# Delta-rule attention with a mixture-of-experts layer: VectorE's side work placed between filter taps, and a merge level of the block inverse in factored form

## The reference, cut to what matters

```python
# x: (8, 1024, 128); q: 8 heads; k, v: 8 heads x 3 householder steps per token; head size 128
q = _short_conv(x @ Wq, conv_q); k = _short_conv(x @ Wk, conv_k); v = _short_conv(x @ Wv, conv_v)
# _short_conv: y[t] = silu(sum of 4 taps w[i] * x[t - 3 + i])
q = _l2norm(q) * d ** (-0.5); k = _l2norm(k)
def step(S, inp):                       # scan over the 1024 tokens
    S = S * jnp.exp(gt)[..., None, None]
    for i in range(nh):                 # 3 rank-1 updates per token
        kS = jnp.einsum('bhd,bhde->bhe', ki, S)
        S = S + bi[..., None, None] * (ki[..., None] * (vi - kS)[:, :, None, :])
    return S, jnp.einsum('bhd,bhde->bhe', qt, S)
o = o * jax.lax.rsqrt(jnp.mean(o * o, -1, keepdims=True) + 1e-05) * rms_weight
x = _layernorm(x + (o * jax.nn.silu(gate)).reshape(b, t, h * dv) @ Wo)
# then a layer of 8 experts with top-2 weights, and a second _layernorm
```

## Time and profile before

| | |
|---|---|
| time, median of 3 runs | 8508.51 us (8502.43 to 8517.87) |
| the profiled execution: own time, span | 8499.04 us, 8497.0 us |
| busy in the span: PE, DVE, ACT, POOL | 7561.9, 6595.7, 5290.1, 4106.0 us |
| mean granted clock of TensorE | 0.956 of full speed |

### The profile page before, as it was taken

One profiled execution on the slowest core, in us unless ns is written; L12 is line 12 of the kernel. 1 busy time (PEld: TensorE's weight loads), 2 busy tenths in 40 slices (PEclk: granted clock), 3 DMA queues, 4 the chain that ended last, 5 costly groups with the idle time before them and its releaser, 6 DMA issues. The chain is left out here.

```text
span 8497.0 us, 425999 instructions
## 1 busy us (share of the span) xinstructions
PE 7561.9 (89%) x155940; PEld 6383.7 (75%) x155940; DVE 6595.7 (78%) x22297; ACT 5290.1 (62%) x19575; POOL 4106.0 (48%) x6333
## 2 busy tenths in 40 slices
PE   5788988888889888888888889889898889979999
PEld 1677777777777777777777777777777777857777
DVE  3888888888888888888888888888888888733333
ACT  2566666666666666666666666666666666623333
POOL 0355555555555555555555555555555555511111
PEclk6799999999999999999999999999999999989999
DMA  2000000000000000000000000000000000010000
GB/s 86 5 9 9 9 10 9 9 9 9 10 9 10 9 9 9 9 10 9 10 10 9 10 9 9 10 8 10 9 9 9 10 9 10 8 29 10 7 10 8
DMA packets 283622, 97.66 MB, mean 11 GB/s; under 512 B 226096, under 2 KB 276544, under 8 KB 281152
## 3 DMA queue, kind: packets, MB, share of 16 engines
q1 hardware_dynamic: 281408, 68.93, 3.7%
HBM read 52.08 MB, written 16.78 MB: 8 GB/s over the span
## 5 line engine op out<-in xcount | busy, mean ns | idle before, releaser
L802 DVE SCALAR_TENSOR_TENSOR CY<-PP,CWV,CY 128x128 f32<-128x128 f32 x4608 | 1590.3, 345 | 102.2 <-ACT CY L721 1.4
L802 DVE SCALAR_TENSOR_TENSOR CY<-PP,CWK,CY 128x128 f32<-128x128 f32 x4608 | 1587.4, 344 | 83.9
L1004 POOL TENSOR_TENSOR UM<-U,C 32x256 f32<-32x256 f32 x1536 | 1104.8, 719 | 120.2 <-POOL UM L1004 20.8
L997 POOL TENSOR_TENSOR Y<-U,C 32x256 f32<-32x256 f32 x768 | 553.9, 721 | 1201.0 <-DVE UQ L880 1160.9
L516 PE MATMUL PP<-XT,WK 128*128 128x131 f32 x3072 | 741.5, 327 | 262.0 <-DVE CY L802 251.5
L516 PE MATMUL PP<-XT,WV 128*128 128x131 f32 x3072 | 756.6, 333 | 239.8 <-DVE CY L802 212.3
L977 POOL TENSOR_TENSOR S<-R,BETA 96x4 f32<-96x4 f32 x512 | 101.4, 198 | 1606.6 <-DVE R L840 1606.6
L536 PE MATMUL PI<-T,WB 32*32 32x32 f32 x49152 | 732.6, 194 | 138.7 <-DVE T L811 133.7
L536 PEld LDWEIGHTS PI<-T,WB 32*32 32x32 f32 x49152 | 623.2, 109 | 298.6 <-issue 230.2
L721 ACT ACTIVATE CY<-PP,CWK 128x128 f32<-128x128 f32 x1536 | 560.7, 365 | 453.8 <-PE PP L516 447.4
L820 DVE SCALAR_TENSOR_TENSOR S<-S,WHOLE,PK 128x128 f32<-128x128 f32 x2048 | 612.6, 341 | 253.1 <-PE PK L591 252.9
(11 more groups left out here) (228 smaller groups left out, 19080.8 us busy)
## 6 DMA issues: line engine op xcount, KB each, us to landing
EX<-exd SPq DMA_DIRECT2D x768, 32.0 KB, 2.2
exd<-EXS SPq DMA_DIRECT2D x16, 512.0 KB, 2.6
XR<-in_L_attn_x SPq DMA_DIRECT2D x65, 64.0 KB, 2.7
XL<-in_L_attn_x SPq DMA_DIRECT2D x16, 256.0 KB, 2.8
XRES<-in_L_attn_x SPq DMA_DIRECT2D x64, 64.0 KB, 3.0
x<-X SPq DMA_DIRECT2D x64, 64.0 KB, 1.6
XI<-x SPq DMA_DIRECT2D x16, 256.0 KB, 2.8
out<-OUT SPq DMA_DIRECT2D x16, 256.0 KB, 2.3
```

The source lines that it names most:

```text
L802: dve.scalar_tensor_tensor(CY[:, m % RING], ptile(m)[:, s:s + P], taps_of(m)[:, s:s + 1], CY[:, m % RING], ALU.mult, ALU.add).then_inc(tap ...
L997: pool.tensor_tensor(Y1[r, :, :], U[r, par, :, r], over(first[r, :], [BK, NHEAD, BK], 1), ALU.mult).then_inc(seed_sb, 1)
L1004: pool.tensor_tensor(UM[r, lv], U[r, par, :, r], over(merge[lv][r, :], [BK, NHEAD, BK], 1), ALU.mult).then_inc(made, 1)
```

## The change

Four things, all in the attention stage.

1. A merge level of the inverse is computed as P = X - N X, Q = N P, result = P + N Q, in place of T0 = X - N X, T1 = X - N T0, result = X - N T1. The matmul blocks are the same in number and size. Q is a plain copy out of PSUM, and ScalarE makes it (steps 2 and 6, ahead of its slot's other work); VectorE keeps steps 1, 3, 5 and 7.
2. VectorE's passes of the inverse move from ahead of tap 1 to between taps 1 and 2, the transposes behind them to between taps 2 and 3. The reciprocal of the row norms moves from behind their sum to between taps 2 and 3. The second half of the state's addition is spread over slots 0 and 1, one head in each gap. QSE moves one gap later.
3. TensorE issues `new_state` in slots 10 and 11 in place of 11 and 12.
4. The norm's work of slot 12 in c = 2 is spread: YL in slot 13, statistics in slots 0 and 1 of c = 3, X1 in slot 4 in place of slot 1. GpSimd's root for it moves from the end of c = 2 to behind the first block of c = 3.

```diff
@@ stage_bufs
-                    "H1": (base, T0, T1),
-                    "H2": (base, T1, (Y2, Y3)[k // 4])}[STAGES[k]]
+                    "H1": (None, T0, T1),
+                    "H2": (T0, T1, (Y2, Y3)[k // 4])}[STAGES[k]]
@@ TensorE's program
-                        if k in (11, 12) and do_run:
-                            new_state(k - 11, run, rc, prep, do_prep)
+                        if k in (10, 11) and do_run:
+                            new_state(k - 10, run, rc, prep, do_prep)
@@ ScalarE's program
-                        if do_inv and k in INV_AT and INV_AT[k] in (0, 4):
+                        if do_inv and k in INV_AT and INV_AT[k] in (0, 2, 4, 6):
                             act.wait_ge(inv_ps, STEPS * invn + INV_AT[k] + 1)
-                            act.activation(WB[:, :, :], inv, ACT.Copy).then_inc(inv_sb, 1)
+                            to = WB if INV_AT[k] in (0, 4) else T1
+                            act.activation(to[:, :, :], inv, ACT.Copy).then_inc(inv_sb, 1)
@@ inv_out
-                    dve.tensor_tensor(to[:, :, :], base[:, :, :], inv, ALU.subtract).then_inc(inv_sb, 1)
+                    dve.tensor_tensor(to[:, :, :], base[:, :, :], inv, ALU.subtract if STAGES[k] == "H" else ALU.add).then_inc(inv_sb, 1)
@@ VectorE's group(i, half, c, k, part)
-                    if k == 0 and known(run - 1, 0, NCH):
-                        add_state(1, run - 1, part)
+                    if do_inv and k in INV_AT and INV_AT[k] not in (0, 2, 4, 6) and part == 0:
+                        inv_out(invn, INV_AT[k])
+                    if do_inv and INV_AT.get(k) == 3 and part == 1:
+                        dve.wait_ge(inv_sb, STEPS * invn + 4)
+                        flip(XB, Y2).then_inc(x2t_sb, 1)
...
+                    if k in (0, 1) and known(run - 1, 0, NCH):
+                        add_state(1, run - 1, 2 * k + part, 4)
                     if k in (3, 5) and do_prep and part == 0:
...
+                    if k in (3, 5) and do_prep and part == 1:
+                        l = k // 5
                         dve.wait_ge(sse_sb, 2 * prep + l + 1)
                         need(dve, kds_sb, 2 * prep - 1 + l)
                         dve.reciprocal(R2[0:R, lanes[l]], SSE[0:R, lanes[l]]).then_inc(r2_sb, 1)
-                    if k == 10 and c == 3 and do_prep and part == 0:
+                    if k == 10 and c == 3 and do_prep and part == 1:
...
-                    if k == 12 and out_now and part == 0:
+                    if k == 13 and out_now and part == 1:
...
-                        dve.wait_ge(y_sb, q + 1)
+                    if k == 0 and norm_now and part == 0:
+                        dve.wait_ge(y_sb, i - 1)
                         dve.bn_stats(ST[:, :], YL[:, :]).then_inc(st_sb, 1)
...
-                    if k == 1 and c == 3 and known(i - 2, 0, NSC) and part == 0:
+                    if k == 4 and norm_now and part == 1:
```

More of the change, by code:

```diff
@@ L459, in stage_bufs @@
             base = (Y1, Y2)[k // 4]
[L460 to L461 removed]
+            return {"W0": (base, None, None), "W1": (base, None, None), "H": (base, base, T0), "H1": (None, T0, T1),
+                    "H2": (T0, T1, (Y2, Y3)[k // 4])}[STAGES[k]]
         def when(i, c):
@@ L826, in group @@
                     ahead, prep, invn, run, do_ahead, do_prep, do_inv, do_run = when(i, c)
+                    norm_now = c == 3 and known(i - 2, 0, NSC)
                     rc, par = (c - 2) % 4, c % 2
@@ L830, in group @@
                     next_x = c == 3 and known(i + 1, 1, NSC)
-                    if k == 0 and known(run - 1, 0, NCH):
-                        add_state(1, run - 1, part)
+                    if do_inv and k in INV_AT and INV_AT[k] not in (0, 2, 4, 6) and part == 0:
[3 more added lines that the diff above has]
+                        flip(XB, Y2).then_inc(x2t_sb, 1)
+                    if do_inv and INV_AT.get(k) == 7 and part == 1:
+                        dve.wait_ge(inv_sb, STEPS * invn + 8)
+                        need(dve, join_ps, 3 * (invn - 1) + 1)
+                        for b in range(2):
+                            r = slice(BK * b, BK * b + BK)
+                            op = dve.transpose(X3[r, :, r], Y3[r, :, :])
+                        op.then_inc(x3t_sb, 1)
+                    if k in (0, 1) and known(run - 1, 0, NCH):
+                        add_state(1, run - 1, 2 * k + part, 4)
                     if k in (3, 5) and do_prep and part == 0:
@@ L881, in group @@
                     if k == 11 and do_run:
-                        add_state(0, run, part)
-                    if k == 12 and out_now and part == 0:
+                        add_state(0, run, part, 2)
+                    if k == 13 and out_now and part == 1:
                         q = i - 2
@@ L911, in program @@
                     for k in range(SLOTS):
-                        if do_inv and k in INV_AT and INV_AT[k] not in (0, 4):
-                            inv_out(invn, INV_AT[k])
-                            if INV_AT[k] == 3:
-                                dve.wait_ge(inv_sb, STEPS * invn + 4)
-                                flip(XB, Y2).then_inc(x2t_sb, 1)
-                            if INV_AT[k] == 7:
-                                dve.wait_ge(inv_sb, STEPS * invn + 8)
-                                need(dve, join_ps, 3 * (invn - 1) + 1)
-                                for b in range(2):
-                                    r = slice(BK * b, BK * b + BK)
-                                    op = dve.transpose(X3[r, :, r], Y3[r, :, :])
-                                op.then_inc(x3t_sb, 1)
                         j, jh, m = lagged(i, half, SLOTS * c + k - 1)
@@ L968, in program @@
                             pool.wait_ge(diag_sb, NBK * run + b + 1)
+                    if c == 3 and known(i - 2, 0, NSC):
+                        pool.wait_ge(mv_sb, 2 * (i - 1))
+                        need(pool, x1_sb, i - 2)
+                        pool.tensor_tensor(RS[:, :], MV[:, 1:2], mhalf[:, 0:1], ALU.pow).then_inc(rs_sb, 1)
                     if c == 2 and known(i - 2, 0, NSC):
@@ L1005, in program @@
                                 pool.wait_ge(made, NBK * prep + b + 1)
-                    if c == 2 and known(i - 2, 0, NSC):
-                        pool.wait_ge(mv_sb, 2 * (i - 1))
-                        need(pool, x1_sb, i - 2)
-                        pool.tensor_tensor(RS[:, :], MV[:, 1:2], mhalf[:, 0:1], ALU.pow).then_inc(rs_sb, 1)
                 pool.wait_ge(ready, READY)
```

12 lines of the change are left out of this document (7 added, 5 removed).

## The result

The changed kernel takes **8429.25 us** (median of 7 runs, 8392.18 to 8454.05) against 8507.31 (7 runs, 8494.94 to 8523.93). The ratio is **0.9908, 95% interval 0.9886 to 0.9929**: faster by 0.9%, where 5.1% was forecast, and 199 us above the upper end of the range. The profiled execution is the median one (own time 8429.25, span 8427.1). Its mean granted clock is 0.934, that of before 0.956.

What follows compares the result with a forecast made beforehand. TensorE was taken to bound T to Y, VectorE Y to T. Savings of 4.2 and 1.9 us plus 0.9 for the clock gave 7.0 per supertile, 434 us over 62 supertiles: 8070 us, range 7920 to 8230.

Steps and rivals of the forecast that it cites:

- the last term: TensorE stretches below full rate after waits for VectorE: about 1.0 us per supertile, 0.9 of it taken as saved.
- what c = 3 has besides: T to Y, c = 3: twice L689 (some 0.8 each), L507 with 0.1, and 1.0 left of a projection's 1.55 wait.
- the copies of Q free: Steps 2 and 6: ScalarE's 8 copies of 0.38 us, 3.0 per supertile, fit its idle time and cost nothing.
- the turn's price: Loop over supertile pairs: 2.9 us of waits per turn, 1.45 per supertile, which the change doesn't touch.
- C: Slot 10: new_state comes too early, waits for ScalarE's copy of the second solve and holds TensorE; 8200 us, chance 0.12.
- D: Steps 2 and 6: ScalarE's copies of Q come late and TensorE stands at the next block; slower, 9070 us, chance 0.05.
- Rival B: T to Y: TensorE's path is shorter than it looks and VectorE alone decides; times below 7930 us, chance 0.10.
- The rule on VectorE: VectorE's pipe is said to empty after every operation, so order would be worth nothing; the trace shows 0.39 against 0.26 us.
- Rival A: Gaps between taps: order is worth nothing by itself, so the 1.9 from Y to T go; 8190 us, chance 0.10.
- the two kinds: Alternating stretches: T to Y, bound by TensorE, saving 4.2 us per supertile; Y to T, bound by VectorE, saving 1.9.

Runs made afterwards that it cites:

- e1: The changed kernel with 5 unused TensorE products added in slot 3 of c = 2, ahead of its wait for T; 8226.05 us, ratio 0.9668.
- e11: The changed kernel with step 1's VectorE pass T alone put back ahead of tap 1; 8245.27 us, ratio 0.9684.
- e7: The changed kernel with FA in slot 3, GpSimd's root between its next work's halves, and unused products (two in c = 2, three in c = 3); 8234.8 us.
- e10: The kernel before with four supertiles per turn of the loop in place of two, nothing else; 8470.87 us, ratio 0.995.
- e4: The changed kernel with the old algebra of the merge level, so the new order alone; 8333.32 us, ratio 0.9776.
- e12: The changed kernel with unused products (five in c = 2, two in c = 3), four supertiles per turn, and T ahead of tap 1; 8052.28 us, ratio 0.9468.
- e2: The changed kernel with FA moved from slot 2 to slot 3, behind T; 8291.62 us, ratio 0.9743.

## Why the prediction was wrong

The direction was right, the size was not: 7.0 us per supertile were forecast, 1.1 came. The mean stretches over those 54 supertiles, from the starts of T and Y, in us (forecast, measured, shortest):

| stretch | forecast | mean | shortest |
|---|---|---|---|
| T to Y, c = 0 | 17.1 | 17.38 | 17.05 |
| T to Y, c = 1 | 17.1 | 17.06 | 17.05 |
| T to Y, c = 2 | 19.9 | **23.37** | 19.85 |
| T to Y, c = 3 | 19.8 | **22.01** | 20.63 |
| Y to T, 0 to 1 | 7.1 | 7.13 | |
| Y to T, 1 to 2 | 7.6 | **8.20** | 8.20 |
| Y to T, 2 to 3 | 7.9 | 7.46 | |
| Y to T, 3 to 0, with the turn's 1.45 | 8.55 | 8.29 | 7.19 |
| sum | 105.1 | 110.9 | |

The sum is 5.8 us over, in 62 supertiles 360 us: 8070 + 360 = 8430, so the table holds the whole error.

**The step that failed** is the last term: "about 1.0 are stretches in which TensorE runs below full rate after waits for VectorE ... Most of the waits ahead of it go (YL), so I take 0.9 of it as saved". Half-rate time over 60 supertiles did not fall to a tenth, it rose from 393 to 737 us. Its size was fair: in the kernel before, 12 of 54 T to Y stretches of c = 3 have some 6.5 us at half rate and last 2.3 us longer than the others, and 29 of 54 from c = 2 to 3 have some and last 0.5 us longer, 0.8 us per supertile in all. What failed is that it would go. I had taken waits as a sum, and counted the ones that go. What e1 and e11 show to matter is where a wait lies: TensorE made faster up to step 1 reaches step 2 early, and idle time that had been scattered over projections lies there in one piece, right ahead of the longest path that TensorE bounds. That is 3.5 us per supertile in c = 2 (23.37 - 19.85), 217 us in all. e1 got back 203 by filling the stand. Whether it matters that the idle time is in one piece, or only that TensorE does so little around it, no run separates. The prediction had the fact at hand, the stretch at 0.79. It asked where VectorE would stand next (before U, T or Y), and never where TensorE would.

**c = 3** is 2.2 over. 1.4 of it is the mean above the shortest. 1.0 of that is the 12 falls (25.67 us against 20.97 for the others, 2.3 us of half rate in the mean stretch); the other 0.3 lies in stretches at full rate, every second of which lasts some 21.4, for a reason that wasn't looked for. The other 0.8 is a mis-sized term: what c = 3 has besides was put at 1.7 plus 1.0 of waiting. The waiting is now 0.3, and the rest 20.63 - 0.27 - 17.06 = 3.3. For c = 2 the same working gave 2.8, and it measures 2.79. Which of c = 3's own matmuls hold the missing 1.6 wasn't tried.

**From c = 1 to 2** the stretch is 8.2 in place of 7.6. FA waits 0.85 us for ScalarE there (52.3 us by 61). In the kernel before it waited a quarter of a microsecond:

```profile
DVE FA L861 <- ACT OGT L734: 14.7, 61, 0.2
```

The difference is 0.6 us per supertile, all that this stretch is over. The prediction costed the order within VectorE, and didn't ask whether ScalarE's input for FA would come earlier too. e7 shows that this term can be moved but not won.

**Right:** the sign; the waits for S and YL gone (229 us to 14 in the whole run for S, 115 to none for YL); new waits of DVE before U and Y, (314.3 - 60.0 + 194.6)/246 = 1.8 per chunk against "1 to 1.5"; T to Y at 17.06 in c = 1 and at its shortest in c = 0, 19.85 in c = 2, 7.13 from c = 0 to 1; the copies of Q free (no wait of TensorE for them appears among its waits); the turn's price (e10). Rivals C and D are out: the waits of TensorE in that window are those for T and for taps, 41.7 us for ScalarE before L558 (25.0 in the kernel before), 15.1 for Y, 3.6 us of issue before L536, and none before `new_state` or for ScalarE's Q. Rival B's times did not come, and its sign was missing too: VectorE does wait for TensorE before U and Y.

**The rule on VectorE.** In the changed kernel's timeline a tap and an S that don't depend on each other start 0.26 us apart (2447.89, 2448.15, 2448.41 below), and the Y to T stretch from c = 0 to 1 fell from 7.66 to 7.13 with the same work in it. Here the prediction read only half of what it cites. The Trainium skill, in "VectorE: DVE Perf Modes", section "The DRAIN you can't avoid", does have the next operation wait for the pipe to empty, but it also says: "A next op that is not held starts earlier". With that sentence the section doesn't make order worthless, and the trace agrees with it: 0.26 where nothing holds the next one, 0.39 where it needs the one before. Rival A is out as well, since the order alone gives 2.2% (e4).

```profile
2447.89 0.34 DVE L803 SCALAR_TENSOR_TENSOR CY<-PP,CWK,CY 128x128 f32<-128x128 f32 x1
2448.15 0.34 DVE L821 SCALAR_TENSOR_TENSOR S<-S,WHOLE,PK 128x128 f32<-128x128 f32 x1
2448.41 0.73 DVE L803 SCALAR_TENSOR_TENSOR CY<-PP,CWK,CY 128x128 f32<-128x128 f32 x2
```

**"T and Y both move behind tap 1, which cancels in the sum of the two kinds"** was right for the sum and hid a choice. Y mostly waits for TensorE anyway (185 waits above), so a tap ahead of it is free. T is waited for, so a tap ahead of it costs 0.38. Moving Y alone wins nearly three of the four such terms, about 1.07 us per supertile (e12), and a shorter stand (e11).

**Where the expected gain went**, then: 434 us forecast; 217 given back through the clock in c = 2, 137 in c = 3 (some 65 with the clock, 20 in the longer stretches at full rate, 50 in the size of its path), 37 before T in c = 2, 17 in c = 0, less 43 in the stretches from c = 2 to 3 and 3 to 0; that leaves some 70, which is the 8499.0 - 8429.3 measured. Filling the stand, keeping T first and halving the turns gives 8052 us, though by another road than the 8070 of the forecast, which didn't count on the turns.

## What to carry to other kernels

When a schedule change frees an engine that is the bound in one stretch and waits in the next, list its idle pieces before and after: a shorter total can be worth less where more of it lies together ahead of the stretch that the engine bounds, because TensorE's clock can fall there and stay down into that stretch. Read the granted clock per stretch, not for the run, and where it falls, fill the stand with unused products (a few lines, 2.4% here) before rebuilding the order. Then read it again, in every stretch: falls can turn up in another one (c = 0 in e1 and e7). And of passes that move together, ask of each whether it waits or is waited for: only the first kind may go behind other work.

## What the runs showed of the hardware

- **Half-rate stretches inside a busy kernel.** In 4 us with 1.94 busy TensorE stood 2.29 in one piece, and then ran at 0.5 (1.2 GHz) for about 10.2 us though it was then busy almost without a gap. The Trainium skill, in "TensorE: Matmul & The Clock Gate", section "What's actually happening", says that the throttled state is the default and that activity releases it. The trace shows the fall, and that the release took its time: over a stretch with 4.00 of 4.00 us busy (2458 to 2462) the clock was still 0.50.
- **It is not certain, and the length of the stand does not decide it alone.** Falls of 10 us or more came in 41 of 54 places behind stands of mostly 2.3 us, in 7 of 54 behind nearly the same in e4 (21 more held 3.4 us at half rate), in 26 of 54 behind 1.9 us (e11), in 12 of 54 behind 1.22 (c = 3 of the changed kernel), in 8 of 54 behind 1.35 (e2), in 7 of 54 behind idle pieces of 0.72 at most (c = 0 of e1), and in none of 54 in c = 2 with the stand filled (e1). What decides between places that look alike stays open. Four runs of one kernel then spread by 91 us (e4), and by 4 us where the T to Y stretches keep the full clock (e12).
- **Unused products cost nothing in a stand**: 2.35 us of them ended as the awaited block began (2487.07), and in the kernel before they changed nothing that could be measured (ratio 0.9994).
- **One turn of the loop costs 2.7 us** here, with all engines in it (e10: 43 us for 16 turns).
